# Attention sums turned by VectorE out of their bank, and weighed two steps behind the scores

## The reference, cut to what matters

```python
s1 = jnp.einsum('bhqd,bhkd->bhqk', q1, k1) * scale      # B=2, H=16, S=2048, d=16
s2 = jnp.einsum('bhqd,bhkd->bhqk', q2, k2) * scale
a1 = jax.nn.softmax(jnp.where(causal, s1, neg_inf), axis=-1)
a2 = jax.nn.softmax(jnp.where(causal, s2, neg_inf), axis=-1)
comb = a1 - lam[None, :, None, None] * a2
out = jnp.einsum('bhqk,bhkv->bhqv', comb, v)            # v has 2*d = 32 columns
normed = (out - mu) * jax.lax.rsqrt(var + LN_EPS)       # per head, over the 32
```

## Time and profile before

| | us |
|---|---|
| median of 3 runs | 1882.6 (1882.38 to 1882.91) |
| the profiled execution, span | 1880.4 |
| TensorE busy | 1850.4 (98%) |
| TensorE weight load busy | 1060.4 (56%) |
| VectorE busy | 1035.6 (55%) |
| ScalarE busy | 1408.3 (75%) |
| GpSimd busy | 229.5 (12%) |

### The profile page before, as it was taken

One profiled execution on the slowest core, in us unless ns is written; L12 is line 12 of the kernel. 1 busy time (PEld: TensorE's weight loads), 2 busy tenths in 40 slices (PEclk: granted clock), 3 DMA queues, 4 the chain that ended last, 5 costly groups with the idle time before them and its releaser, 6 DMA issues.

```text
span 1880.4 us, 30846 instructions
## 1 busy us (share of the span) xinstructions
PE 1850.4 (98%) x12172; PEld 1060.4 (56%) x12172; DVE 1035.6 (55%) x2005; ACT 1408.3 (75%) x1702; POOL 229.5 (12%) x308
## 2 busy tenths in 40 slices
PE   8999999999999999999999999999999999999997
PEld 6774333333333333333333335888888888888886
DVE  5566566556655665566556655454545454636343
ACT  5549999999999999999999997454545454544452
POOL 3002111211121112111211121000000000000000
PEclk9999999999999999999999999999999999999999
DMA  8777634663466346634663411000010100000000
GB/s 270 263 259 163 113 67 78 116 111 64 82 115 116 59 82 116 116 63 78 116 104 73 80 53 43 26 12 34 12 34 12 34 12 34 12 34 23 1 12 14
DMA packets 130673, 146.11 MB, mean 78 GB/s; under 512 B 74756, under 2 KB 100996, under 8 KB 122884
## 3 DMA queue, kind: packets, MB, share of 16 engines
q1 hardware_dynamic: 128936, 139.32, 33.8%
q10 hardware_dynamic: 1584, 4.72, 0.7%
HBM read 101.79 MB, written 39.06 MB: 75 GB/s over the span
## 4 chain that ended last, share of the span: by engine, by line
PE 92%; DVE 5%; issue 1%; DMA 0%; ACT 0%; SPq 0%; DVEq 0%; PEldq 0%
PE attn_sums_ps L1104 27%; PE split_hid_ps L1716 25%; PE attn_s_ps L1079 20%; PE split_hid_ps L1700 6%; PE proj_qk_ps L545 3%; PE split_y_ps L1733 3%; PE proj_v_ps L555 2%; PE split_y_ps L1656 2%; PE attn_sums_ps L1112 2%; PE split_turn_ps L1644 1%; DVE attn_raw L1252 1%; DVE attn_raw L1241 1%; DVE attn_sums_sb L1236 0%; DVE attn_diff L1261 0%; DVE proj_xt_low L424 0%
## 5 line engine op out<-in xcount | busy, mean ns | idle before, releaser
L1041 ACT ACTIVATE attn_probs<-attn_s_ps 128x1024 f32<-128x1024 f32 x1088 | 1002.5, 1122 | 6.9 <-PE attn_s_ps L1079 6.3
L1104 PE MATMUL attn_sums_ps<-attn_probs,heads_v 128*32 128x512 f32 (+3 forms) x5120 | 586.3, 539 | 0.1
L1079 PEld LDWEIGHTS attn_s_ps<-heads_q,heads_k 50*128 50x128 f32 x2560 | 211.7, 184 | 434.5 <-ACT attn_probs L1041 376.6
L1079 PE MATMUL attn_s_ps<-heads_q,heads_k 50*128 50x512 f32 (+3 forms) x2560 | 449.7, 426 | 0.0
L1810 ACT ACTIVATE split_whole<-split_hid_ps,scales 128x512 f32<-128x512 f32 x128 | 88.3, 690 | 274.3 <-PE split_hid_ps L1716 274.1
L1022 POOL TENSOR_SCALAR_AFFINE_SELECT attn_probs<-attn_probs 128x512 f32<-128x512 f32 x256 | 176.7, 702 | 832.2 <-ACT attn_probs L1041 832.2
L1716 PE MATMUL split_hid_ps<-split_hid_b,ffn_r 128*128 128x512 f32 x1024 | 240.8, 392 | 0.0
L1716 PE MATMUL split_hid_ps<-split_hid_a,ffn_r 128*128 128x512 f32 x1024 | 237.9, 391 | 0.0
L1716 PEld LDWEIGHTS split_hid_ps<-split_hid_a,ffn_r 128*128 128x128 f32 x1024 | 190.0, 188 | 41.0 <-DVE split_hid_a L1985 1.3
L1716 PEld LDWEIGHTS split_hid_ps<-split_hid_b,ffn_r 128*128 128x128 f32 x1024 | 189.8, 188 | 38.2
L1104 PEld LDWEIGHTS attn_sums_ps<-attn_probs,heads_v 128*32 128x32 f32 x5120 | 107.6, 108 | 174.0 <-issue 139.3
(11 more groups left out here) (182 smaller groups left out, 1682.0 us busy)
## 6 DMA issues: line engine op xcount, KB each, us to landing
heads_q_raw<-qk_raw SPq DMA_DIRECT2D x60, 384.0 KB
heads_k_raw<-qk_raw SPq DMA_DIRECT2D x60, 384.0 KB
qk_raw<-proj_copies SPq DMA_DIRECT2D x64, 256.0 KB, 2.5
values<-proj_v SPq DMA_DIRECT2D x8, 1024.0 KB, 6.5
heads_k_raw<-ones SPq DMA_DIRECT2D x60, 128.0 KB
heads_v<-values SPq DMA_DIRECT2D x15, 512.0 KB, 19.0
heads_spare<-in_ffn SPq DMA_DIRECT2D x30, 256.0 KB, 9.7
split_heads<-diffs SPq DMA_DIRECT2D x7, 1024.0 KB, 5.2
```

The costliest lines, as they stand in the source:

```text
L1041: nc.scalar.activation(weights, side_by_side, ACT.Exp, scale=SCALE).then_inc(exp_done, 1)
L1079: last = nc.tensor.matmul(s_ps[(NU * h + n) % SLOTS][:, s, col:col + width], k_sb[u][rows, b * SEQ + j * PARTS:b * SEQ + (j + 1) * PARTS], ...
L1104: last = nc.tensor.matmul(sums[c * D:(c + 1) * D, off:TILE], v_sb[u][:, b * KEY_BLOCKS + j, :], probs[k % PROBS][:, b, s, place:place + wi ...
```

## The change

- VectorE turns a tile's sums itself: one transpose of 32x32 blocks straight from the bank to `raw` (`take_sums`). It takes the place of the copy, TensorE's four transposes and the second copy. The wait on `turned` and its semaphores go.
- For this the bank is laid out another way. The four matmuls of a block are now one for each batch b and each r in 0, 1, where r picks every other run of 32 queries, of both softmaxes at once. Each still takes as many columns as before; it reads them in runs of 32 with a gap of 32 and writes two runs of up to 256.
- `raw`, `recip`, `total` and `diff` change layout to fit; `finish_tile` has the same five operations of the same sizes. `store_rows` stores from 64 partitions with twice the runs for each.
- `LAG` is 2 in place of 3: the weighing of step k-2 follows the scores of step k. All that hangs on a weighing in `EARLY` moves with it.
- `square_heads` goes. In head 15 the rows of heads 0 to 14 come back from DRAM as before and are squared and summed there (`sum_known`, four times two operations of 128x480). Head 15's own rows of tile 0 no longer lie where they are needed: SyncE stores them (`store_first`) and loads them back before VectorE's `early_var`.
- The last tile's `turn` and second copy go from the finishing stage; only `finish_tile` is left there.

```diff
-    LAG = 3
-    TURN_LAG = 2
+    LAG = 2
...
+            def store_first(h):
+                sp.wait_ge(diff_ready, NT * h + 1)
+                store_rows(h, 0, 0, GROUPS, first_stored)
...
+                    store_first(h)
+                    sp.wait_ge(first_stored, 16)
+                    sp.dma_start(early["heads"][:, :, KNOWN:KNOWN + D], diffs[0:SUBS].rearrange("s p h d -> p s (h d)")[:, :, KNOWN:KNOWN + D]).then_inc(heads_whole, 16)
...
                 for j, off, width, place in laid(k):
                     for b in range(BATCH):
-                        for s in range(2):
-                            c = 2 * b + s
-                            last = nc.tensor.matmul(sums[c * D:(c + 1) * D, off:TILE], v_sb[u][:, b * KEY_BLOCKS + j, :], probs[k % PROBS][:, b, s, place:place + width],
+                        alternate = probs[k % PROBS][:, b, :, place:place + width].rearrange("p s (g r n) -> p s g r n", r=2, n=D)
+                        for r in range(2):
+                            c = 2 * b + r
+                            both = sums[c * D:(c + 1) * D, :].rearrange("p (s n) -> p s n", s=2)[:, :, off // 2:HALF_TILE]
+                            last = nc.tensor.matmul(both, v_sb[u][:, b * KEY_BLOCKS + j, :], alternate[:, :, :, r, :],
                                                     start=(j == 0), stop=(k == END[t] and j == blocks[-1]))
...
-            def turn(h, t):
-                pe.wait_ge(sums_copied, NT * h + t + 1)
-                for i in range(SUBS):
-                    last = nc.tensor.transpose(sums_ps[t % 2][:, i * PARTS:(i + 1) * PARTS], sums_sb[:, i * PARTS:(i + 1) * PARTS], keep["ident"][:, :])
-                last.then_inc(turned, 1)
...
                 weigh(h, u, k)
-                if k - TURN_LAG in END:
-                    turn(h, END.index(k - TURN_LAG))
-                elif k - TURN_LAG + NS in END and not first:
-                    turn(h - 1, END.index(k - TURN_LAG + NS))
...
-            def copy_sums(h, t):
-                n = NT * h + t
+            def take_sums(h, t):
                 dve.wait_ge(probs_free, PROBS + NS * h + END[t] + 1)
-                dve.wait_ge(turned, n + 1)
-                nc.vector.tensor_copy(sums_sb[:, :], sums_ps[t % 2][:, :]).then_inc(sums_copied, 1)
-            def take_turned(h, t):
-                dve.wait_ge(turned, n + 2)
-                nc.vector.tensor_copy(raw[:, :, :, :].rearrange("p k s d -> p (k s d)"), sums_ps[t % 2][:, :]).then_inc(sums_bank_free, 1)
+                nc.vector.transpose(raw[:, :, :, :].rearrange("p s g d -> p (s g d)"), sums_ps[t % 2][:, :]).then_inc(sums_bank_free, 1)
...
                 sum_counts()
                 tile(h, 0)
-                square_heads(h)
+                early_wo()
+                for s in range(SUBS):
+                    sum_known(s)
                 early_var()
-                early_wo()
-                copy_sums(h, 1)
                 early_rstd()
                 early_norm(0)
                 early_norm(1)
-                take_turned(h, 1)
-                finish_tile(h, 1)
+                tile(h, 1)
```

More of the change, by code:

```diff
@@ L849, in attention_programs @@
     D = VALUE_DIM
+    HALF_TILE = TILE // 2
+    GROUPS = TILE // (2 * D)
+    ROWS = BATCH * D
     VEC = 5
@@ L944, in sync_program, with store_rows, store_ahead @@
         def sync_program(sp):
-            def store_rows(h, rows, done):
-                for b in range(BATCH):
[L948 to L954, removed]
+            def store_rows(h, b, begin, end, done):
+                to = diffs[b * KEY_BLOCKS:(b + 1) * KEY_BLOCKS, :, h, :].rearrange("k (g p) n -> p (k g) n", p=ROWS)
+                sp.dma_start(to[:, begin:end, :], diff[b * ROWS:(b + 1) * ROWS, begin:end, :]).then_inc(done, 16)
+            def store_first(h):
+                sp.wait_ge(diff_ready, NT * h + 1)
+                store_rows(h, 0, 0, GROUPS, first_stored)
+            def store_ahead(h, last):
+                sp.wait_ge(diff_ready, NT * h + NT - 1)
+                for b in range(BATCH):
+                    store_rows(h, b, GROUPS if last and b == 0 else 0, LAST_GROUPS, ahead_stored)
             def store_rest(h):
                 sp.wait_ge(diff_ready, NT * h + NT)
-                store_rows(h, slice(LAST_ROWS, KEY_BLOCKS), stored)
+                for b in range(BATCH):
+                    store_rows(h, b, LAST_GROUPS, NT * GROUPS, stored)
             def load_half(n):
@@ L999, in head @@
                 load_half(2 * h)
-                store_ahead(h)
+                store_ahead(h, last)
                 load_half(2 * h + 1)
@@ L1178, in tensor_program @@
             use(LAST, LAST % 2, False, NS - 1)
-            def late():
-                turn(LAST, NT - 1)
-            if_wide(pe, wide, "tensor", late, late, lambda: pe.wait_ge(wide_loaded, 16 * CHUNKS))
+            if_wide(pe, wide, "tensor", None, no_part, lambda: pe.wait_ge(wide_loaded, 16 * CHUNKS))
         def vector_program(dve, exact):
@@ L1245, in finish_tile @@
                 v0 = VEC * n
-                rows = diff[:, SUBS * BATCH * t:SUBS * BATCH * (t + 1), :]
-                sums = raw[:, :, :, :].rearrange("p k s d -> p (k s) d")
+                rows = diff[:, GROUPS * t:GROUPS * (t + 1), :]
+                sums = raw[:, :, :, :].rearrange("p s g d -> p (s g) d")
                 dve.wait_ge(sums_bank_free, 2 + n + 1)
@@ L1402, in last_head, with late @@
                 early_xt(1)
-                copy_sums(h, 3)
-            def late(part):
-                if part == 0:
-                    take_turned(LAST, NT - 1)
-                else:
-                    finish_tile(LAST, NT - 1)
-            def late_all():
-                late(0)
-                late(1)
+                take_sums(h, NT - 1)
+            def late():
+                finish_tile(LAST, NT - 1)
             def rest_of_first():
@@ L1689, in tile @@
                 pair = hid_ps[2 * (m % 2):2 * (m % 2) + 2]
-                if split and not prior and m == 2:
-                    late()
                 if m < 2:
@@ L1987, in tile @@
             if split and not prior:
-                late(1)
+                late()
             for layer, hid in enumerate((hid_b, hid_a)):
```

67 lines of the change are left out of this document (34 added, 33 removed).

## The result

| | before | after |
|---|---|---|
| median, us | 1882.76 (1882.38 to 1882.98) | 1902.76 (1901.45 to 1902.92) |
| span of the profiled execution, us | 1880.4 | 1900.9 |
| TensorE busy, us | 1850.4 | 1840.5 |
| VectorE busy, us | 1035.6 | 980.7 |
| ScalarE busy, us | 1408.3 | 1409.8 |

The change makes the kernel slower, by a ratio of 1.0103 (95% interval 1.009 to 1.0116). The forecast was 1903.4, and the range 1884 to 1914. The lines have moved: the exponentials are L1051 (L1041 before), the scores L1089 (L1079), the weighing L1116 (L1104), the masks L1032 (L1022), and VectorE's transpose is L1230.

What follows compares the result with a forecast made beforehand. ScalarE's exponentials were taken to bound the kernel. Heads 1 to 14, head 0, head 15 and the finishing stage sum as 18.1 + 2.2 + 0.9 - 0.4 = +20.8, taking 1882.6 to 1903.4 us; range 1884 to 1914.

Steps and rivals of the forecast that it cites:

- The turns' gain: TensorE's transposes go: up to 0.33 us a head, 5.0 at most over 15 heads, and 0.4 in the finishing stage.
- The stall per pair, m - 0.90: Stall at mask pairs of steps 2, 9, 31; m runs from the pair's last exponentials to its last mask's end.
- The release of 0.15: Time from the end of GpSimd's masks to the start of TensorE's weighing: 0.15 us.
- rival 1: The masks' wait is covered, only the gain from removing TensorE's transposes is left: about 1877.5 us; chance 12%.
- rival 2: Stalls at one pair in three, or a release near 0.05, with the transposes' gain: 1879 to 1890 us; chance 8%.
- Heads 1 to 14: +18.1: Middle heads each pay stalls of 0.66 + 0.48 + 0.48 = 1.62 us in place of 0.33, 1.29 more.
- Pair 31: Step 31's masks: the CAST moves ahead of them, m falls to 1.38, stall 0.48; otherwise m 2.09, stall 1.19.
- Rival 4: Step 31's masks stay slow (+10.7, 1914 us), or head 15's VectorE chain comes late (2 to 5); chance 10%.
- Head 0: +2.2: VectorE's opening work stretches step 2's masks to m = 2.28, stall 1.38; plus 0.48 + 0.48, less 0.15 lost now.
- Head 15: +0.9: Last head: +0.2 up to its `project` blocks, +0.7 for the chain with `turn_mid` before step 35's scores.
- The costs set at nothing: VectorE's transpose (0.69 us, hidden), 64-partition stores, head 15's added VectorE operations (5.6 us) and the interleaved matmul reading: no cost.
- Rival 3: The interleaved matmul operand is slower: at 0.25 a full weighing, 2.7 us a head, +43, about 1945 us; chance 8%.

Runs made afterwards that it cites:

- the split wait: Changed kernel, LAG still 2, with each diagonal block's matmuls waiting for their own mask instead of all masks of the step: 1879.29 us, ratio 0.9979.
- the first experiment: Changed kernel with LAG back at 3, VectorE's transpose and the new bank layout kept: 1876.99 us, ratio 0.9967 against the kernel before.
- the second experiment: Kernel before with LAG 2 alone, TensorE's transposes and both copies kept: 1914.46 us, ratio 1.0166 against the kernel before.

## Why the prediction was right

**The bound.** ScalarE's pace bounds a head: 62.33 in the kernel at three steps' distance and with the split wait, with ScalarE busy all of it. Confirmed.

**The turns' gain.** The first experiment has all of it: 877.33 - 872.73 = 4.6 over 14 heads, 0.33 each as taken. Confirmed. In the kernel before, the 0.33 stand at steps 5, 8, 12 and 26, whose exponentials end 0.11, 0.15, 0.05 and 0.03 late; in the first experiment none of them is late. The 0.4 of the finishing stage is not shown: the -0.46 measured is no larger than the spread between profiles of the same stage.

**The stall per pair, m - 0.90.** Confirmed at three values of m. m = 0.96 left 0.2 a head, m = 1.39 gave 0.49 or 0.50 at each pair, and m = 1.79 gave 0.9. The release of 0.15, taken from a single place in head 0, held throughout: in after, 63 of the 64 pairs' weighings start 0.14 or 0.15 behind their masks, and the last, pair 17 of head 15, starts 1.54 behind them. With that rival 1 fell, and rival 2 too. That pairs 2, 9 and 31 stall and pair 17 doesn't is also as forecast: beyond the clean pace, the exponentials of steps 5, 12 and 34 end 0.50, 0.49 and 0.49 late. Nothing is late behind pair 17, though its masks are the longest, 1.41, and there is no fourth stall.

One of the signs was wrong. I had the weighing start right behind a mask at pairs 2, 9 and 31 "and nowhere else", but it does so at pair 17 as well:

```profile
693.31 1.07 PE L1116 MATMUL attn_sums_ps<-attn_probs,heads_v 128*32 128x384 f32 x16 [0.25 <-POOL attn_probs L1032]
```

The prediction's own working had this wait (1.71 against 1.40); it said rightly that ScalarE doesn't feel it.

**Heads 1 to 14: +18.1, measured +16.7.** The term that was mis-sized is pair 2's m. VectorE's row of `round_half`'s CAST beside pair 2, and of the CAST beside pair 17:

```profile
665.90 0.69 DVE L1212 CAST ffn_r<-heads_spare 128x512 fp32r<-128x512 f32 x1
...
691.76 0.90 DVE L572 CAST heads_spare<-heads_q_raw 128x512 fp32r<-128x512 f32 x1
```

The first began at 665.90, about 0.2 after the second mask had (two masks from 665.10, 1.23 in all). The masks were not lengthened; the CAST took 0.69 in place of 0.43. The second began with the first mask, at 691.76, and the masks took 1.41. I had the CAST some 0.4 behind the masks' start, where it was 0.8, and gave it the price of the second case: m = 1.56, stall 0.66. It was 1.39 and 0.50. That is 0.16 x 14 = 2.2 less. The rest of the difference is of the other sign. The two other stalls came to 0.49 in place of 0.48. And heads 1, 5 and 12 take 0.24, 0.10 and 0.29 more than the other middle heads, where before only heads 5 and 12 did, by 0.08 and 0.11; why is open.

The rule of the Trainium skill that was weighed there (SBUF — State Buffer, Who interferes with whom) says that where such a cast and an operation of GpSimd's meet, whichever issues first holds the ports that they share for its whole instruction, and the other waits. The prediction's 0.91 priced only the case of VectorE first. Here the mask was first and the CAST waited, 0.69 in place of 0.43, so the trace agrees with the rule; what was wrong was to apply it to this pair the other way round.

**Pair 31.** Its masks took 1.23 in place of 1.93, because cutting had ended and the CAST ran at 712.71, 4.7 before them. The second experiment is the counter-proof: the same distance with TensorE's turns has m = 1.79 there. Rival 4 fell.

**Head 0: +2.2, measured +2.7.** Step 2's masks are 2.12 long as before. The term most off is pair 9, taken as elsewhere, m = 1.38. In after m is 1.76 in this head:

```profile
166.66 1.23 POOL L1032 TENSOR_SCALAR_AFFINE_SELECT attn_probs<-attn_probs 128x512 f32<-128x512 f32 x2 [1.57 <-ACT attn_probs L1051]
```

The masks are 1.23 long but start 0.53 after the exponentials in place of 0.16, with VectorE idle. By the formula this is 0.4 more, and the exponentials of step 12 do end 0.87 late. The late start, 0.52 or 0.53, stands in head 0 of all seven profiles of the experiments on the changed kernel, and neither before nor in the second experiment (0.17). It thus comes with the change; why is open. A second term was off by 0.1: I took off 0.15 as lost in head 0 before, but its 62.46 are only 0.02 above the first experiment's 62.44.

**Head 15: +0.9, measured +0.7.** `turn_mid` before the scores of step 35 costs 1.37, as the experiment that moves it back shows. The distance of two steps gives back 0.86, since one weighing fewer is left behind the last scores: from the last exponentials to the last weighing's end it is 2.87 before and in the first experiment (three steps' distance), and 2.01 in after and in all others at two. That is +0.5 for the chain, where I had +0.7 (its own figures give 0.63). With `turn_mid` moved back, head 15 takes 69.74 against 69.58 before: +0.2 for the rest, as taken.

**The costs set at nothing.** The transpose takes 0.717 us against the 0.69 taken, one pass over the bank. The estimate of 1.24 from the Trainium skill's figure for a quarter of the size in bf16 (VectorE: DVE Perf Modes, The three transpose paths) was not borne out. The interleaved operand costs nothing: 604 ns in both, and 1.00 from a weighing to the next scores (678.88 to 679.88). Rival 3 fell. In head 15 VectorE's eight added operations took 5.5 us from first to last. They held up no `turn_heads`: the waits of ScalarE's that go with the four `project` blocks are 1.15, 1.28, 1.27 and 1.28 in after, and 1.16, 1.28, 1.28 and 1.28 in the second experiment, which doesn't have these operations.

## What to carry to other kernels

Before work is moved closer behind its producer, follow the whole chain of the tightest step, here exponentials, two masks, release, weighing, next scores. Compare it with the slack that the order of steps gives there, not with an average. A chain that is too long by half a microsecond at three places a head costs more than taking 38 us of transposes off TensorE brings. Where one wait stands for several results, look whether it can be split by what each consumer reads: that alone gave back 23 us here.

## What the runs showed of the hardware

**ScalarE's idle time understates its waiting.** In the first experiment, back-to-back ACTIVATEs of 128x1024 mostly start 0.903 and end 0.917 apart, while the recorded length of one grows in an unbroken run from about 1.07 up to 1.58. The mean is 1275 ns in the first experiment, 1176 in after, and 1122 before, so it is no measure of waiting either. Between the two kernels the idle time differs by 21.1 us (5.4 and 26.5), and the time to the last exponentials by 27.7, of which 1.2 is the start. Periods between like events measure the loss; idle time does not.

**Who comes first.** A CAST on VectorE that met GpSimd's masks already running took 0.69 or 0.90 in place of 0.43. It lengthened two masks of 1.22 by 0.2 where it began with the first of them, and not where it began within the second. The same two places look alike in every middle head of after; no run was made for it alone. With VectorE ahead the masks pay more: in the kernel before, a CAST begun just before pair 31's masks, which start at 704.76, and the operation behind it made 1.93 of their 1.22. VectorE there:

```profile
704.74 0.43 DVE L572 CAST heads_spare<-heads_q_raw 128x512 fp32r<-128x512 f32 x1
705.20 1.00 DVE L574 SCALAR_TENSOR_TENSOR heads_q<-heads_spare,query_rows,heads_q_raw 128x512 fp32r<-128x512 f32 x1
```

**A releaser can be named wrongly.** In the second experiment the wait before pair 31's weighing is put down to ScalarE; the wait ends 0.15 behind GpSimd's masks and 1.94 behind ScalarE.
